# Expert layer of a small language-model tower on one core: the second expert product over both batches at once

## The reference, cut to what matters

```python
grouped = x.reshape(B, S // t, t, D)                                   # t = 16, D = 128
cont_logits = einsum('bgtd,des->bgtes', grouped, controller) + tie
cont_perm = (cont_logits == max(cont_logits, axis=-3, keepdims=True))
intermediate = einsum('bgtd,desf->bgtesf', grouped, f1)                # F = 32
inner = relu(einsum('bgtesf,bgtes->bgesf', intermediate, cont_perm))
inter2 = einsum('bgesf,esfd->bgesd', inner, f2)
result = einsum('bgesd,bgtes->bgtd', inter2, cont_perm)
h = h + result
```

## Time and profile before

| What | Value |
|---|---|
| median of three runs | 501.92 us |
| the profiled execution | 501.19 us, of which the span (first to last instruction) is 499.4 us |
| attention and what stands ahead of it | up to about 455 us of the span |
| expert stage, up to the last residual add | about 455 to 497.2 us of the span |
| PE busy / weight loads busy | 96% / 80% of the span |
| DVE / ACT / POOL busy | 80% / 73% / 46% of the span |

### The profile page before, as it was taken

How to read it: one execution, slowest core, us unless ns; L and a number is a source line. 1 busy time by engine, 2 the same in 40 slices (tenths; PEclk the granted TensorE clock), 3 DMA queues, 4 the chain that set the end, 5 groups by cost and what they waited for, 6 DMA issues and landing times.

```text
span 499.4 us, 11296 instructions
## 1 busy us (share of the span) xinstructions
PE 478.2 (96%) x3936; PEld 398.5 (80%) x3936; DVE 398.6 (80%) x738; ACT 363.9 (73%) x688; POOL 231.1 (46%) x226
## 2 busy tenths in 40 slices
PE   2999999999999999999999999999999999999887
PEld 2955788888888888888788888888888888888775
DVE  5469999878887887788887888788878899989455
ACT  1258788888788778877888688878887788683543
POOL 1112586667346734663246735663566345541000
PEclk9999999999999999999999999999999999999999
DMA  6500019432943295361612592349234933000002
GB/s 234 211 1 0 2 44 214 92 86 58 195 95 84 48 194 108 85 137 43 127 62 66 109 194 52 81 99 197 53 84 90 194 66 84 1 1 3 3 13 76
DMA packets 29483, 44.78 MB, mean 90 GB/s; under 512 B 3200, under 2 KB 21120, under 8 KB 29184
## 3 DMA queue, kind: packets, MB, share of 16 engines
q1 hardware_dynamic: 28864, 44.21, 37.6%
q10 hardware_dynamic: 576, 0.00, 0.1%
HBM read 6.46 MB, written 1.05 MB: 15 GB/s over the span
## 4 chain that ended last, share of the span: by engine, by line
PE 90%; DVE 5%; DMA 2%; ACT 2%; issue 1%; SPq 0%; POOL 0%; DVEq 0%; ACTq 0%
PE ps L686 24%; PE ps L670 22%; PE ps L654 11%; PE ps L655 11%; PE ps L596 5%; PE ps L729 3%; PE ps L591 2%; PE ps L658 2%; DMA arena<-in_wqkv_rows 2%; PE ps L877 2%; PE ps L860 2%; PE ps L891 1%; DVE pt_lo L1351 1%; DVE neg_max L1363 1%; PE ps L566 1%; PE ps L842 1%
## 5 line engine op out<-in xcount | busy, mean ns | idle before, releaser
L431 POOL TENSOR_SCALAR probs<-probs,inv_sum 128x1024 f32<-128x1024 f32 x128 | 144.8, 1131 | 184.3 <-DVE inv_sum L1357 181.6
L1363 DVE TENSOR_REDUCE neg_max<-ps 128x1 f32<-128x1024 f32 x128 | 156.6, 1223 | 63.9 <-PE ps L658 63.8
L1026 ACT ACTIVATE pt_hi<-ps 128x512 fp32r<-128x512 f32 x256 | 139.2, 595 | 39.7 <-PE ps L670 39.6
L1351 DVE TENSOR_TENSOR pt_lo<-ps,pt_hi 128x512 fp32r<-128x512 f32 x256 | 162.3, 676 | 1.5 <-ACT pt_hi L1026 1.5
L686 PE MATMUL ps<-pt_hi,v_slot 128*128 128x256 f32 x512 | 150.2, 326 | 0.0
L1046 ACT ACTIVATE probs<-ps,neg_max 128x1024 f32<-128x1024 f32 x128 | 142.5, 1113 | 1.5 <-DVE neg_max L1363 0.7
L670 PE MATMUL ps<-ident,probs 128*128 128x128 f32 x1024 | 133.8, 274 | 0.7 <-DVE v_all L1271 0.6
L686 PE MATMUL ps<-pt_lo,v_slot 128*128 128x256 f32 x512 | 127.7, 281 | 0.0
L670 PEld LDWEIGHTS ps<-ident,probs 128*128 128x128 f32 x1024 | 110.1, 141 | 1.3 <-DVE v_all L1271 0.7
L686 PEld LDWEIGHTS ps<-pt_hi,v_slot 128*128 128x128 f32 x512 | 96.6, 189 | 9.7 <-issue 9.7
L686 PEld LDWEIGHTS ps<-pt_lo,v_slot 128*128 128x128 f32 x512 | 96.8, 189 | 8.8 <-issue 8.8
(11 more groups left out here) (141 smaller groups left out, 404.8 us busy)
## 6 DMA issues: line engine op xcount, KB each, us to landing
q_st<-arena SPq DMA_DIRECT2D x28, 256.0 KB, 3.7
k_hi<-arena SPq DMA_DIRECT2D x28, 256.0 KB, 5.1
k_lo<-arena SPq DMA_DIRECT2D x28, 256.0 KB, 5.3
v_slot<-v_all SPq DMA_DIRECT2D x14, 512.0 KB, 3.9
arena<-arena SPq DMA_DIRECT2D x28, 256.0 KB, 5.4
f_sb<-in_f SPq DMA_DIRECT2D x2, 1024.0 KB, 10.7
x<-in_tok SPq DMA_DIRECT2D x2, 512.0 KB, 7.8
w_slot<-in_w_pairs SPq DMA_DIRECT2D x8, 128.0 KB, 2.1
```

The source lines that it names most:

```text
L431: pool.tensor_scalar(probs[:, t % 4, :], probs[:, t % 4, :], inv_sum[:, t % 4:t % 4 + 1], 1.0, ALU.mult, ALU.mult).then_inc(norm_done, 1)
L1026: act.activation(dst, ps[:, transposes_bank(t, a, drain), :].rearrange("p (j c) -> p j c", c=P), ACT.Copy).then_inc(hi_done, 1)
L1351: dve.tensor_tensor(pt_lo[at], ps[:, transposes_bank(t, a, drain), :].rearrange("p (j c) -> p j c", c=P), pt_hi[at].bitcast(F32), ALU.subt ...
L1363: dve.tensor_reduce(neg_max[:, t % 4:t % 4 + 1], ps[:, SCORES + 2 * (t % 2):SCORES + 2 * (t % 2) + 2, :].rearrange("p a c -> p (a c)"), AX ...
```

## The change

The second expert product is done once for both batches. `hidden` becomes one tile, laid out so that the 64 columns of batch 0 and the 64 of batch 1 stand side by side for every k; `inter_t` becomes one tile over the whole of `v_flat`. `second_product(c)` runs in four groups c = 0 to 3, each of 4 values of k by 4 row tiles, so 16 matmuls of 128 columns (x32 in the records). Even groups write banks 0 to 3, odd ones banks 4 to 7; group c waits for the copies of group c - 2. A copy still moves 128x512, now in runs of 4 elements, and reads PSUM with a step of 128 elements in place of 64. The row transposes of n alternate between banks 0, 1 and banks 6, 7, and the first waits for the copies of all four groups.

```diff
-        hidden = [probs_flat[:, SEQ * b:SEQ * (b + 1)].rearrange("p (k g) -> p k g", g=PAIRS) for b in range(B)]
+        hidden = probs_flat[:, 0:2 * SEQ].rearrange("p (k b g) -> p k b g", b=B, g=PAIRS)
...
-        inter_t = [a.rearrange("p (g e) -> p g e", e=ES) for a in experts_of]
+        inter_t = v_flat.rearrange("p (g e) -> p g e", e=ES)
...
-        ROW_BANKS = [0, 0, 0, 0, PV_BANK, 0, PV_BANK, 0]
+        ROW_BANKS = [0, PV_BANK, 0, PV_BANK, 0, PV_BANK, 0, PV_BANK]
...
+        def inter_parts(c, q):
+
+            first = NK * q + 4 * c
+            return (inter_t[:, :, first:first + 4],
+                    ps[:, INTER_BANKS[c % 2] + q, :].rearrange("p (k g) -> p g k", k=4))
...
+            def second_product(c):
+
+                if c == 0:
                     pe.wait_ge(hid_left, 3)
                     pe.wait_ge(hid_right, 1)
-                if half == 1:
-                    inter_copied(2 * b)
-                for k in range(8 * half, 8 * half + 8):
+                if c >= 2:
+                    inter_copied(c - 2)
+                for k in range(4 * c, 4 * c + 4):
                     for q in range(4):
                         rows = slice(F * q, F * (q + 1))
-                        ins = pe.matmul(ps[:, INTER_BANKS[b] + q, k % 8 * PAIRS:(k % 8 + 1) * PAIRS], f2_sb[rows, k, :],
-                                        hidden[b][rows, k, :], start=True, stop=True, tile_position=(F * q, 0))
+                        ins = pe.matmul(ps[:, INTER_BANKS[c % 2] + q, 2 * PAIRS * (k % 4):2 * PAIRS * (k % 4 + 1)],
+                                        f2_sb[rows, k, :], hidden[rows, k, :, :], start=True, stop=True,
+                                        tile_position=(F * q, 0))
                 ins.then_inc(int_mm, 1)
...
                 b, g = ROWS[n]
-                if g == 0:
-                    inter_copied(2 * b + 1)
+                if n == 0:
+                    inter_copied(3)
...
             first_product(0)
-            second_product(0, 0)
             choice_transposes(1)
             take(1, 0)
-            second_product(0, 1)
             take(1, 1)
+            first_product(1)
+            for c in range(4):
+                second_product(c)
             row_transposes(0)
-            first_product(1)
-            results(0)
-            row_transposes(1)
-            second_product(1, 0)
-            results(1)
-            row_transposes(2)
-            second_product(1, 1)
-            results(2)
-            row_transposes(3)
-            for n in range(3, 8):
+            for n in range(8):
                 if n < 7:
                     row_transposes(n + 1)
                 results(n)
...
-            inter_copies(0, 0)
             dve.wait_ge(permt_mm, 4)
             dve.tensor_copy(*choice_parts(1, 1)).then_inc(chosen_done, 1)
-            take_copy(0, 2)
-            take_copy(0, 3)
-            inter_copies(0, 1)
-            take_copy(1, 2)
-            take_copy(1, 3)
-            row_copy(0)
+            for r in range(2):
+                for j in range(2, 4):
+                    take_copy(r, j)
             dve.wait_ge(hid_mm, 4)
             dve.tensor_scalar(*hidden_parts(1, 1), 0.0, None, ALU.max).then_inc(hid_right, 1)
...
+            for c in range(4):
+                inter_copies(c)
+            row_copy(0)
+            for n in range(8):
                 if n < 7:
                     row_copy(n + 1)
                 add_residual(n)
```

More of the change, by code:

```diff
@@ L301, in hidden_parts @@
         def hidden_parts(b, half):
-            return hidden[b][:, 8 * half:8 * half + 8, :], ps[:, HIDDEN_BANKS + half, :].rearrange(
+            return hidden[:, 8 * half:8 * half + 8, b, :], ps[:, HIDDEN_BANKS + half, :].rearrange(
                 "p (k g) -> p k g", g=PAIRS)
[L306 to L310, removed]
+        def inter_parts(c, q):
+            first = NK * q + 4 * c
+            return (inter_t[:, :, first:first + 4],
+                    ps[:, INTER_BANKS[c % 2] + q, :].rearrange("p (k g) -> p g k", k=4))
         def row_parts(n, side):
@@ L846, in first_product, with inter_copied @@
                         ins.then_inc(hid_mm, 1)
[L848 to L852, removed]
+            def second_product(c):
+                if c == 0:
                     pe.wait_ge(hid_left, 3)
                     pe.wait_ge(hid_right, 1)
-                if half == 1:
-                    inter_copied(2 * b)
-                for k in range(8 * half, 8 * half + 8):
+                if c >= 2:
+                    inter_copied(c - 2)
+                for k in range(4 * c, 4 * c + 4):
                     for q in range(4):
                         rows = slice(F * q, F * (q + 1))
-                        ins = pe.matmul(ps[:, INTER_BANKS[b] + q, k % 8 * PAIRS:(k % 8 + 1) * PAIRS], f2_sb[rows, k, :],
-                                        hidden[b][rows, k, :], start=True, stop=True, tile_position=(F * q, 0))
+                        ins = pe.matmul(ps[:, INTER_BANKS[c % 2] + q, 2 * PAIRS * (k % 4):2 * PAIRS * (k % 4 + 1)],
+                                        f2_sb[rows, k, :], hidden[rows, k, :, :], start=True, stop=True,
+                                        tile_position=(F * q, 0))
                 ins.then_inc(int_mm, 1)
-            def inter_copied(n):
-                pe.wait_ge(int_left, 2 * n + 2)
-                pe.wait_ge(int_right, 2 * n + 2)
+            def inter_copied(c):
+                pe.wait_ge(int_left, 2 * c + 2)
+                pe.wait_ge(int_right, 2 * c + 2)
             def row_transposes(n):
                 b, g = ROWS[n]
-                if g == 0:
-                    inter_copied(2 * b + 1)
+                if n == 0:
+                    inter_copied(3)
                 for side in range(2):
                     for j in range(PPT):
-                        first = 2 * (NT * j + 2 * g + side)
+                        first = 2 * (b * NT * PPT + NT * j + 2 * g + side)
                         ins = pe.transpose(ps[:, ROW_BANKS[n] + side, j * P:(j + 1) * P],
-                                           inter_t[b][:, first:first + 2, :].rearrange("p u e -> p (u e)"), ident[:, :])
+                                           inter_t[:, first:first + 2, :].rearrange("p u e -> p (u e)"), ident[:, :])
                     ins.then_inc(intp_mm, 1)
@@ L1081, in rectify, with inter_copies @@
                 act.activation(*hidden_parts(b, half), ACT.Relu).then_inc(hid_left, 1)
-            def inter_copies(b, half):
-                act.wait_ge(int_mm, 2 * b + half + 1)
+            def inter_copies(c):
+                act.wait_ge(int_mm, c + 1)
                 for q in range(2):
-                    act.activation(*inter_parts(b, half, q), ACT.Copy).then_inc(int_left, 1)
+                    act.activation(*inter_parts(c, q), ACT.Copy).then_inc(int_left, 1)
             def row_copy(n):
@@ L1103, in _ @@
             rectify(0, 1)
-            inter_copies(0, 0)
             choice_copy(1, 0)
-            take_copy(1, 0, 0)
-            take_copy(1, 0, 1)
-            inter_copies(0, 1)
-            take_copy(1, 1, 0)
-            take_copy(1, 1, 1)
-            row_copy(0)
-            rectify(1, 0)
[L1113 to L1117, removed]
+            for r in range(2):
+                for j in range(2):
+                    take_copy(1, r, j)
+            rectify(1, 0)
+            for c in range(4):
+                inter_copies(c)
+            for n in range(8):
                 row_copy(n)
```

6 lines of the change are left out of this document (3 added, 3 removed).

## The result

The changed kernel takes 503.16 us (median of 20 runs, 502.60 to 505.70), the kernel before 501.81 us beside it (20 runs). The ratio is 1.0035, with a 95% interval of 1.0024 to 1.0047: 1.35 us more of the median, or 0.27% (a ratio in this document is estimated from the single runs of both kernels, and is not the quotient of their medians). That lies within the 0.5% called no change, 0.8 us above the forecast of 502.4 us.

A forecast was written before the change was run, and what follows sets the result against it. PE was taken to bound the stage, with waits for DVE second. PE's 3.8 us saving is given back in six gaps, net +0.4 us: 501.6 us profiled, 502.4 us on the median's footing, range 500.9 to 505.0 us.

The forecast's parts named there:

- the price of the products: Second product on PE: 128 instructions of 128 columns at about 31 ns each, as in take.
- the cycle: PE's closing steady alternation of one row_transposes and one results, 1.60 us each, up to results(7) near 496.5.
- the waits for the copies: DVE's copies stand in the chain of waits where PE's products stood; row_transposes(0) near 484.0 waits for them.
- a granted clock under 1.00 between 470 and 496 us: Listed sign, in the expert stage on PE, that the forecast is wrong.
- What PE saves: Second product: 256 instructions at 30.5 ns (7.8 us) become 128 at 31.3 ns (4.0 us), saving 3.8 us.
- What the new order exposes: From first_product(0)'s end to results(7): steps wait for one another, six gaps give back the saving, sum +0.4 us.
- The copies: Second product's copies in runs of 4 elements: no change taken; rival that they double, +4.8 us, 507.2 us, chance 0.04.
- The wait called issue: PE wait without releaser, 1.22 us before: taken as 0, or +1.22 between first_product(1) and the copies.
- The clock: Rival: PE's clock falls in waits ahead of first_product(1) and row_transposes(0), slower, 505.6 us, chance 0.10.
- Two times of 1.6 us: Clock rival's price: two low-clock spells of 1.6 us on PE, 3.2 us on top of 502.4.
- It decides from the point where the waits reach what lay behind 496.68: Clock rival's threshold: PE's clock fell after some 1.3 to 1.8 us without work; new order has two 1.4 us waits.
- PE's saving shows in full: Rival: copies run under the products, so the end moves by the 3.8 us, 498.1 us, chance 0.08.

The follow-up runs named there:

- wide fill: Changed kernel with 5 unread matmuls of 256 or 512 columns in PE's gaps around the takes and first_product(1): 502.61 us, ratio 1.0013.
- narrow product: Changed kernel's order, second product over 64 columns of one batch per matmul: 512.27 us, ratio 1.0190; also with free banks and early first group: 509.47 us, 1.0100.
- free banks: Changed kernel with take(1, 1) writing banks 0 to 3, so it waits for no copy: 500.97 us, ratio 0.9989.
- early first group: Changed kernel with group 0 waiting only for the ReLU of the first halves of hidden: 503.62 us, ratio 1.0036.
- shifted blocks: 12 unread small matmuls (48 instructions) ahead of first_product(0); on the changed kernel with free banks and early first group: 500.15 us, ratio 0.9967.
- the woven kernel with the choices first: Kernel before with batch 1's choice transposes and copies ahead of second_product(0, 0): 500.99 us, ratio 0.9987; with the 48 instructions: 499.75 us, ratio 0.9961.
- the wide one: Changed kernel with free banks, early first group and 12 unread small matmuls (48 instructions) ahead of first_product(0): 500.15 us, ratio 0.9967.

## Why the prediction was right, point by point

The forecast was no change in the sense of 0.5%, by a saving on PE that new waits give back. That is what came, and the range held the median, if not every run: three of the 20 lie above 505.0. Part of that is luck. The waits came as forecast, but so did the fall of the clock, which had been given a chance of 0.10, and the range was wide enough for what it cost. By its own list the account is mixed: the price of the products, the cycle and the waits for the copies are signs of being right, a granted clock under 1.00 between 470 and 496 us is one of being wrong, and it is there. Measured from the start of `first_product(0)`:

| start of | forecast | full clock (wide fill) | changed kernel, profiled |
|---|---|---|---|
| `choice_transposes(1)` | 1.92 | 1.93 | 1.92 |
| `take(1, 0)` | 3.76 | 3.80 | 3.80 |
| `first_product(1)` | 8.95 | 8.99 | 9.65 |
| group 0 | 11.85 | 11.97 | 14.14 |
| `row_transposes(0)` | 18.28 | 18.81 | 20.67 |
| `results(7)` | 30.77 | 31.23 | 33.09 |

- *What PE saves.* The price of the wide instruction was right: the weight loads are as long, and the 64 of groups 0 and 1 run in 2.07 us, the last one's latency included. The saving is real, 2.1 to 3.0 us at a full clock by the one run that shows it; where the narrow product loses its clock the difference is larger.
- *What the new order exposes.* Each wait is there, at its place and nearly its size: 0.78 for the choices, 1.49 ahead of `row_transposes(0)`; from group 0 to `row_transposes(0)` 6.53 us were measured where 6.43 were forecast. With a full clock the order follows the forecast to 0.12 us up to group 0. Of the 0.4 us by which `row_transposes(0)` is then late, 0.3 are the slow start of group 0 in that profile (2.38 in place of 2.07 us).
- *The copies.* No change of price was forecast, and none came; that rival is out.
- *The wait called issue.* Taken at 0, with 1.22 as the other end. The profiles of the changed kernel show none of it, probably since `first_product(1)` takes 3.5 us at the lower clock and leaves the block time to arrive. But it came back in kernels of this order whose clock was full there, with 0.65 and 1.41 us, so that the upper end was well kept. How much of it stands in the changed kernel's own runs with a full clock is open, as none was profiled. By the page "Runtime: NRT & Kernel Launch" of the Trainium skill ("Instruction fetch mechanics") such a fetch is mostly hidden. For most blocks of this stage the traces agree (in the kernel before, five packets ran between 465 and 490 us and one wait called issue of over 0.3 us stood), but not for all: 0.65 to 1.55 us stood in the timeline of PE in six kernels.
- *The clock.* This is the term that was mis-sized. It had a chance of 0.10 and counted as a full clock in the forecast; in 17 of the 20 runs the mean is at 0.997 or less, and both profiles put the fall in the stage. Two times of 1.6 us were named as its price, and 504.55 - 502.62 = 1.9 us is what the long spell costs. The ten runs at 0.997 are 0.5 us above those with a full clock; the one of this kind that was profiled has a short spell. Of the 1.35 us, then, some 0.8 are in the runs with a full clock (502.62 us against 501.81; 1.0013 with the wide fill), for which the forecast had 0.4, and the rest is the clock's. The step that failed is "It decides from the point where the waits reach what lay behind 496.68": the clock fell behind gaps of 0.78 and 0.76 us in one profile and of 1.35 us in the other, and stayed up over one of 1.84 us in the kernel with the free banks. The length of one gap is not what it goes by; what it does go by stays open. The place was right, or nearly: the thin stretch around the takes, ahead of `first_product(1)` or at its start.
- *PE's saving shows in full.* That rival did not come true. The nearest is another kernel: with free banks, an early first group and shifted blocks the wide product is 1.7 us faster than before (ratio 0.9967), under half of the 3.8 us, and it took three edits more.

## What to carry to other kernels

Making a product cheaper for PE by merging two halves also takes away the work that covered the copies around them: write down, for each step of the new order, which copy it waits for and what PE does meanwhile, and give the waiting step free banks before anything else (about 2 us here, a part of it by way of the clock). Look at the granted clock of the stretch itself and not at its mean over the kernel, 0.993 here for a product that took 3.59 in place of 1.99 us. And where a wait has no releaser in the profile, count instructions: if it stands at the same count in several versions, moving the count can be worth more than the edit under study. It is not sure to: the same 48 instructions went with the two fastest kernels here and won nothing in the kernel before.

## What the runs showed of the hardware that was not expected

- The granted clock can fall while PE's record is busy without a break: 0.50 from 482 to 486 us with 2.00 of 2.00 us busy in each row, in matmuls of 64 columns by 32x128 weights in four row tiles (the narrow product); with 128 columns, behind the same steps and with a wait of 0.60 us in the middle, it stayed at 1.00 (480 to 485 us). One of 31 runs of the kernel before in the third set has the same mean clock, 0.983, and took 510.41 us; where its clock fell isn't shown.
- Work that nobody needs may save time: with ten instructions in the gaps the ratio is 1.0013 where it was 1.0035 and 1.0047 (three sets), while 34 for the same purpose brought 1.0052, with 1.41 us of issue inside a dense product.
- The clock can fall in stretches that no edit touched: in the profiles of two kernels it was at 0.50 from 34 to 36 us, in the attention, at a mean of 0.996, and three runs with such a mean took some 2 us longer than the other nine of their kernel.
- Such a wait kept its distance in instructions across kernels (936, 682, 684, and 888 with 48 put ahead), and each such wait ended 2.2 to 2.7 us behind the start of a block's packet on the instruction queue (478.5 to 480.70 us in the kernel before). With 48 instructions put ahead the packet came in time in the woven kernel with the choices first (475.4 us) and in the wide one (472.2, with the block's end at about 476.0), and late in the kernel before (479.7); what sets the time of the packet stays open.
